# Graph network layer on one core: comparing dst rows group by group, and stores of the counts issued by ScalarE

## The reference

```
# layer 0: a message per edge, summed by dst
msg = relu(concat(x[dst], x[src], edge_attr, u) @ W1 + b1)
agg = segment_sum(msg, dst)
x   = layernorm(x + relu(concat(x, agg, u) @ W2 + b2))
# layers 1 and 2 (same edges)
h   = x @ W + b
agg = segment_sum(h[src] + edge_attr @ We + be, dst) + h
x'  = batchnorm(relu(agg) + bias)
# end
out = layernorm(x + layer 2 of layer 1 of x)
```

## Time and profile before

| | |
|---|---|
| median of 3 runs | 8024.89 us (8016.9 to 8026.22) |
| profiled execution, its own time | 8035.52 us |
| its span | 8033.7 us |
| mean granted TensorE clock | 0.78 |
| preparation, to the first sum of a tile | 0 to 266 us |
| tiles and counts | 266 to 4741 us |
| windows to nodes | 4741 to about 5390 us |
| layers 1 and 2 | about 5390 to 8034 us |

### The profile page before, as it was taken

How to read it: one execution, slowest core, us unless ns; L and a number is a source line. 1 busy time by engine, 2 the same in 40 slices (tenths; PEclk the granted TensorE clock), 3 DMA queues, 4 the chain that set the end, 5 groups by cost and what they waited for, 6 DMA issues and landing times.

```text
span 8033.7 us, 166672 instructions
## 1 busy us (share of the span) xinstructions
PE 6117.4 (76%) x60411; PEld 5242.1 (65%) x60411; DVE 4457.3 (55%) x5988; ACT 2089.5 (26%) x5280; POOL 3990.2 (50%) x3983
## 2 busy tenths in 40 slices
PE   3136777777777777777777747779999999999996
PEld 2025555555555555555555536679999999999996
DVE  2238888888888888888888838860011111001113
ACT  1014444444444444444444400000000000000001
POOL 3777777777777777777777754430011110001111
PEclk9996666666666666666666665569999999999998
DMA  5227777777777777777777764449999998999996
GB/s 117 54 61 223 246 240 243 250 242 251 247 242 244 249 249 246 247 246 242 248 252 244 248 175 149 151 170 382 380 363 382 382 382 345 378 361 382 382 384 247
DMA packets 973642, 2113.96 MB, mean 263 GB/s; under 512 B 668464, under 2 KB 758534, under 8 KB 859646
## 3 DMA queue, kind: packets, MB, share of 16 engines
q1 hardware_dynamic: 814200, 1844.92, 61.7%
q0 software_dynamic: 137664, 259.86, 13.6%
q10 hardware_dynamic: 21696, 8.08, 0.6%
HBM read 1457.70 MB, written 654.73 MB: 263 GB/s over the span
## 4 chain that ended last, share of the span: by engine, by line
PE 49%; DVE 19%; issue 12%; DMA 9%; POOL 8%; DVEq 1%; SPq 1%; ACT 1%; ACTq 0%; POOLq 0%
PE psum L947 25%; PE psum L836 10%; DVE edge_area L1322 9%; POOL arena L669 5%; PE psum L811 4%; PE psum L794 4%; DMA arena<-adj 4%; PE psum L795 2%; DVE arena L1313 2%; POOL arena L683 2%; DMA arena<-in_src_steps 1%; DVE edge_area L1327 1%; DMA arena<-b_tab,arena 1%; POOL arena L641 1%; DMA arena<-q_tab,m_window 1%
## 5 line engine op out<-in xcount | busy, mean ns | idle before, releaser
L669 POOL DMA_INDIRECT arena<-b_tab,arena x3125 | 3122.2, 999 | 952.2 <-issue 935.8
L1322 DVE TENSOR_TENSOR edge_area<-psum,arena 128x1024 bf16<-128x1024 f32 x2368 | 2484.6, 1090 | 622.1 <-PE psum L811 622.1
L1075 ACT CAST arena<-psum 128x392 bf16<-128x392 f32 x4736 | 1921.2, 505 | 2119.9 <-PE psum L811 2066.5
L947 PE MATMUL psum<-arena 128*128 128x192 bf16 x29008 | 2449.4, 246 | 29.0 <-DMA arena<-adj 20.7
L947 PEld LDWEIGHTS psum<-arena 128*128 128x128 bf16 x29008 | 2403.2, 98 | 38.3 <-issue 35.0
L811 PE MATMUL psum<-edge_area 64*128 64x98 bf16 x18944 | 1226.7, 241 | 464.9 <-ACT arena L1075 456.3
L794 PE MATMUL psum<-w_edge,arena 96*128 96x288 f32 x1250 | 677.3, 638 | 957.8 <-DVE arena L1313 957.8
L731 POOL DMA_INDIRECT arena<-a_carry,a_carried x196 | 185.0, 944 | 2404.3 <-DVE arena L1512 1374.5
L811 PEld LDWEIGHTS psum<-edge_area 64*128 64x128 bf16 x18944 | 782.6, 110 | 712.0 <-issue 684.7
L1478 DVE TENSOR_REDUCE arena<-psum 128x64 f32<-128x192 f32 x296 | 104.1, 352 | 1700.2 <-PE psum L947 1114.6
L794 PEld LDWEIGHTS psum<-w_edge,arena 96*128 96x128 f32 x1250 | 268.2, 267 | 1035.4 <-issue 1035.4
(11 more groups left out here) (248 smaller groups left out, 3263.7 us busy)
## 6 DMA issues: line engine op xcount, KB each, us to landing
arena<-adj SPq DMA_DIRECT2D x592, 1568.0 KB, 8.8
adj<-arena SPq DMA_DIRECT2D x296, 1568.0 KB
q_tab<-arena SPq DMA_DIRECT2D x312, 480.0 KB, 3.4
edge_area<-q_tab SPq DMA_DIRECT2D x117, 768.0 KB, 5.0
arena<-in_edge_t_steps SPq DMA_DIRECT2D x312, 192.0 KB
over_area<-q_tab SPq DMA_DIRECT2D x78, 768.0 KB
arena<-b_tab,arena POOLq DMA_INDIRECT x3125
over_area<-m_cont SPq DMA_DIRECT2D x196, 48.0 KB
```

Source lines behind the costliest of these rows:

```text
L669: nc.gpsimd.indirect_dma_start(rows[:, us, k, S - 1 - s, :], None, b_tab[:, :], bass.IndirectOffsetOnAxis(ap=index[:, us, 1 - k, s:s + 1], ...
L947: one = mm(psum[:, h, 0:3 * F], ring[:, r, n, :], xs[l][:, k, :], start=(k == 0 and not own), stop=(k == NB - 1))
L1075: copy(stage[:, h2, h, :, column:column + BATCH], psum[:, 2 + 2 * b + h, 0:BATCH * NB].rearrange("p (e n) -> p n e", n=NB)).then_inc(kept, 1)
L1322: one = V.tensor_tensor(to[:, d, :, :], over(lanes, [P, HOT, n], 1), over(code, [P, HOT, n], 2), ALU.is_equal)
```

## The change

Three things. DVE's preparation starts with the compares, unrolled, and puts the other parts behind single groups: the ends behind group 2, the masks behind 3 and 4, the flags behind 6, the products behind 7 and 8. PE makes the shift of the ends ahead of its own group 6 and turns the flags ahead of group 12, not behind all 14 groups. And the eight stores of counts in a cycle are issued by ACT, behind its copies of an odd step, not by SP; SP's loop loses them and one peeled cycle.

```diff
 # SP
-            def store_quarter(q, h, part): ... sp.wait_ge(kept, ...); sp.dma_start(adj..., stage...)
-            def store_quarters(c, uu, build_now, built_before): ...
             def tile_cycle(c):
 ...
                     over_unit(c, uu)
-                    store_quarters(c, uu, build_now, built_before)
-            tile_cycle(0, False, False)
-            tile_cycle(1, True, False)
-            with sp.Fori(2, BUILD + 1) as c:
-                tile_cycle(c, True, True)
+            tile_cycle(0)
+            with sp.Fori(1, BUILD + 1) as c:
+                tile_cycle(c)
 # PE
             for g in range(NG):
                 h = g % 2
+                if g == 6:
+                    shift_ends()     # waits for ends_known; 8 products, ends_ps_done
+                elif g == 12:
+                    turn_conts()     # waits for conts_known; 3 transposes, conts_turned
                 pe.wait_ge(xt_in[h], 16 * (g // 2 + 1))
 ...
-            pe.wait_ge(ends_known, 1)
-            ...                      # the same 8 products and 3 transposes
 # ACT
+            quarters_at = ((0, 1), (2,), (3,), ())
+            def store_quarter(q, h, part):
+                of, half = part // 2, slice(part % 2 * QH, (part % 2 + 1) * QH)
+                act.wait_ge(kept, q * (2 * PAIR_BATCHES) + 2 * PAIR_BATCHES)
+                act.dma_start(adj[of][some(q, 1), :, half.start * P:half.stop * P]...,
+                             stage[:, h, of, half, :]...).then_inc(adj_out[h], 16)
+            def store_quarters(c, uu, build_now, built_before):
+                if uu >= 4 and build_now:
+                    for part in quarters_at[uu - 4]:
+                        store_quarter(c * 2 - 2, 0, part)
+                if uu < 4 and built_before:
+                    for part in quarters_at[uu]:
+                        store_quarter(c * 2 - 3, 1, part)
             def keep_cycle(c, build_now=True, built_before=True):
                 for j in range(CYCLE):
                     if build_now:
                         keep_batches(c, j)
                     over_step(c, j)
+                    if j % 2:
+                        store_quarters(c, j // 2, build_now, built_before)
 # DVE
-            dve.wait_ge(dst_in, 64)
-            ...                      # ends, masks, dve.wait_ge(ends_ps_done, 1), flags, products
-            counted_loop(dve, count, 0, NG // 2, compare)
+            for g in range(NG):
+                compare(g)
+                if g == 2:
+                    ends_of_windows()          # waits for dst_in
+                elif g == 3:
+                    run_mask(m_mask, m_dst, m_ends, MOB, WM)
+                elif g == 4:
+                    run_mask(a_mask, a_dst, a_ends, AOB, WA)
+                elif g == 6:
+                    continuations()            # waits for ends_ps_done
+                elif g == 7:
+                    run_goes_on(m_mask, m_cond, MOB, WM)
+                elif g == 8:
+                    run_goes_on(a_mask, a_cond, AOB, WA)
```

More of the change, by code:

```diff
@@ L454, in _ @@
             sp.dma_start(a_cont[1:1 + AOB * P].rearrange("(b p) -> b p", p=P), cont_t[0:AOB, 2, :]).then_inc(conts_out, 16)
[L456 to L468, removed]
             q_windows = q_tab.rearrange("(w i) f -> w (i f)", i=WM)
             units_of = ((0, 1), (1, 2, 3), (3, 4), (4, 5, 6), (6, 7))
-            quarters_at = ((0, 1), (2,), (3,), ())
             def load_over(c, n):
@@ L522, in over_unit, with tile_cycle @@
                     load_cont(c, 3)
-            def tile_cycle(c, build_now, built_before):
+            def tile_cycle(c):
                 for uu in range(CU):
@@ L536, in tile_cycle @@
                     over_unit(c, uu)
-                    store_quarters(c, uu, build_now, built_before)
             sp.wait_ge(conts_out, 80)
-            tile_cycle(0, False, False)
-            tile_cycle(1, True, False)
-            with sp.Fori(2, BUILD + 1) as c:
-                tile_cycle(c, True, True)
-            tile_cycle(CYCLES - 1, False, True)
+            tile_cycle(0)
+            with sp.Fori(1, BUILD + 1) as c:
+                tile_cycle(c)
+            tile_cycle(CYCLES - 1)
             us = (UNITS - 1) % 4
@@ L758, in _, with shift_ends, turn_conts @@
             pe.wait_ge(globals_kept, 1)
+            def shift_ends():
+                pe.wait_ge(ends_known, 1)
+                for at, of, n in ((0, m_ends[:, 0, :], MOB), (MOB, m_ends[:, 1, :], MOB),
+                                  (2 * MOB, a_ends[:, 0, :], AOB), (2 * MOB + AOB, a_ends[:, 1, :], AOB)):
+                    mm(ends_ps[:, at:at + n], shift[:, :], of[:, 0:n], start=True, stop=False)
+                    one = mm(ends_ps[:, at:at + n], wrap[:, :], of[:, 1:n + 1], start=False, stop=True)
+                one.then_inc(ends_ps_done, 1)
+            def turn_conts():
+                pe.wait_ge(conts_known, 1)
+                nc.tensor.transpose(glob_ps[0:NB, 0:P], m_cont_p[:, 0:NB], ident[:, :])
+                nc.tensor.transpose(glob_ps[0:NB, P:2 * P], m_cont_p[:, NB:2 * NB], ident[:, :])
+                nc.tensor.transpose(glob_ps[0:AOB, 2 * P:3 * P], a_cont_p, ident[:, :]).then_inc(conts_turned, 1)
             for g in range(NG):
                 h = g % 2
+                if g == 6:
+                    shift_ends()
+                elif g == 12:
+                    turn_conts()
                 pe.wait_ge(xt_in[h], 16 * (g // 2 + 1))
@@ L1096, in over_step, with keep_cycle @@
                     over_keep(b + (j - 10) // 3)
-            def keep_cycle(c, build_now=True):
+            quarters_at = ((0, 1), (2,), (3,), ())
+            def store_quarter(q, h, part):
+                of, half = part // 2, slice(part % 2 * QH, (part % 2 + 1) * QH)
+                act.wait_ge(kept, q * (2 * PAIR_BATCHES) + 2 * PAIR_BATCHES)
+                act.dma_start(adj[of][some(q, 1), :, half.start * P:half.stop * P].rearrange("k p n -> (k p) n"),
+                             stage[:, h, of, half, :].rearrange("p n c -> p (n c)")).then_inc(adj_out[h], 16)
+            def store_quarters(c, uu, build_now, built_before):
[5 more added lines that the diff above has]
+                        store_quarter(c * 2 - 3, 1, part)
+            def keep_cycle(c, build_now=True, built_before=True):
                 for j in range(CYCLE):
@@ L1102, in keep_cycle @@
                     over_step(c, j)
+                    if j % 2:
+                        store_quarters(c, j // 2, build_now, built_before)
             act.wait_ge(codes_kept, AP_ // 2)
             act.wait_ge(codes_turned, AP_ // 2)
-            keep_cycle(0, False)
-            keep_cycle(1)
+            keep_cycle(0, False, False)
+            keep_cycle(1, True, False)
             with act.Fori(2, BUILD + 1) as c:
@@ L1262, in _, with ends_of_windows @@
-            counted_loop(dve, count, 0, NG // 2, compare)
+            def ends_of_windows():
+                dve.wait_ge(dst_in, 64)
+                for of, ends, n in ((m_dst, m_ends, MOB), (a_dst, a_ends, AOB)):
+                    note(V.tensor_copy(ends[:, 0, 0:n], of[:, :, 0]))
+                    note(V.tensor_copy(ends[:, 1, 0:n], of[:, :, of.shape[2] - 1]))
+                count.wait()
+                V.tensor_scalar(m_target[:, :], m_ends[:, 1, 0:MOB], 0.0, None, ALU.max).then_inc(ends_known, 1)
@@ new lines, in run_mask, with continuations @@
+            def run_mask(mask, of, ends, n, w):
+                note(V.tensor_tensor(mask[:, 0:n, :], of, over(ends[:, 1, 0:n], [P, n, w], 2), ALU.is_equal))
+            def continuations():
+                dve.wait_ge(ends_ps_done, 1)
+                note(V.tensor_tensor(m_cond, ends_ps[:, 0:MOB], m_ends[:, 1, 0:MOB], ALU.is_equal))
+                note(V.tensor_tensor(m_cont_p, ends_ps[:, MOB:2 * MOB], m_ends[:, 1, 0:MOB], ALU.is_equal))
+                note(V.tensor_tensor(a_cond, ends_ps[:, 2 * MOB:2 * MOB + AOB], a_ends[:, 1, 0:AOB], ALU.is_equal))
+                V.tensor_tensor(a_cont_p, ends_ps[:, 2 * MOB + AOB:2 * (MOB + AOB)], a_ends[:, 1, 0:AOB], ALU.is_equal)\
+                    .then_inc(conts_known, 1)
@@ new lines, in run_goes_on, with compare @@
+            def run_goes_on(mask, cond, n, w):
+                count.wait()
+                note(V.tensor_tensor(mask[:, 0:n, :], mask[:, 0:n, :], over(cond, [P, n, w], 2), ALU.mult))
+            def compare(g):
+                h = g % 2
+                wait(dve, rows_compared, g)
+                dve.wait_ge(tile_rows_in[h], (g // 2 + 1) * (16 * GB))
+                link(V.tensor_tensor(is_less, tile_rows[:, h, :, :],
+                                     over(node[:, g * GB:(g + 1) * GB], [P, GB, P], 2), ALU.is_lt))
+                V.tensor_reduce(t[5][:, g * GB:(g + 1) * GB], is_less, AX.X, ALU.add).then_inc(rows_compared, 1)
```

## The result

The changed kernel takes 8075.99 us (median of 4 runs, 8072.17 to 8080.99) against 8025.56 us (8016.9 to 8028.64, 4 runs): a ratio of 1.0065, its 95% interval 1.0048 to 1.0082. It is slower by 50 us where 64 us less had been forecast, and far outside the range of 7940 to 7995.

What follows compares the result with a forecast made beforehand. POOL's list of gathers was taken to pace the first 4740 us, its 78 us hole paid in full. Compares first gained 64 us, stores on ACT 0: 8024.9 - 64 = 7961 us, range 7940 to 7995.

Steps and rivals of the forecast that it cites:

- Part 1: Preparation, compares first: POOL's gap before group 2 closes and source gathers start at 168.4 us, 64.0 us earlier.
- 105.0 us from group 1 to the source gathers: Preparation: 84 unhindered gathers at 1.25 us each, following group 1, so source gathers could start at 154.0 us.
- the holds: Preparation: DVE's four long operations now run beside POOL's gathers and hold them up, 8.2 to 13.2 us, taken as 12.4.
- the two more microseconds: Preparation: DVE's compares hold up POOL's gathers, bounds 0 to 17.5 us, taken as 2.
- Group 0 was in time: Preparation: group 0's rows might land as late as 54.28 us, costing POOL 7.5 us; taken as 0.
- 8.8 us for the compares: Preparation: by the skill page's contention rule every compare could hold a gather, 8.8 us, a gain of 57, not 64.
- Part 2: Count stage: ACT issues the stores in place of SP; bounds -17 to +136 us, taken as 0.
- The landings: Count stage: with stores in their own queue gathers land later; DVE would wait 4.1 us more, once, giving 7965.
- the queues served in turns: DMA engines take turns between busy queue rows; a third would give gathers every third turn in place of every second.
- POOL as the pace: First 4740 us: POOL gathers without a pause and sets the pace, so a hole in its list is paid in full.
- Rival 1: Count stage: ACT's store issues delay its copies, then PE and DVE; full price 136 us, 8097 us; chance 0.05.
- The signs that I named for part 2 going wrong: Count stage: ACT's idle after steps 5 and 11 near 0, DVE's idle before line 1322 longer, POOL waiting for sums or indices.

Runs made afterwards that it cites:

- earlier: Changed kernel, stores still on ACT, but each half's last quarter issued behind steps 3 and 11 instead of 5 and 13; 7955.17 us, ratio 0.9913 to the kernel before.
- stores_only: Kernel before with only the stores moved to ACT (SP and ACT as changed, PE and DVE as before); 8134.25 us, ratio 1.0136.
- half1_earlier: Changed kernel with only the second half's last quarter store moved from behind step 5 to behind step 3; 7968.17 us, ratio 0.9936 to the kernel before.
- sp_ahead: Kernel before with the new preparation, stores on SP, the second half's last quarter directly ahead of the window's load; 8075.57 us, ratio 1.0065.

## Why the prediction was wrong

**Part 1, right in each of its terms.** The 105.0 us from group 1 to the source gathers, the holds and the two more microseconds gave 168.4; measured 168.15. The four long operations held 2.96 + 3.27 + 3.21 + 3.27 = 12.7 us (the rows of 72.72 to 125.67 less 0.94 each); I took 12.4. Group 0 was in time: its compare started at 44.10, ahead of the 54.28 of the bound. For the compares I took 2 us: POOL started 0.24 us earlier than before (31.15 against 31.39), 154.0 - 0.24 + 12.7 = 166.5, and 1.7 us remain to 168.15. The page "GPSIMD Engine Reference" of the Trainium skill, section "8. Key points", says that POOL's SBUF interfaces contend with DVE's instructions of two SBUF inputs; the prediction made 8.8 us for the compares of it. The trace bears it out for all four long operations, and for the compares in small part (the 1.7 us).

**Part 2, the step that failed.** I wrote of SP's eight issues that in "a cycle from SP, whose DMAs nobody in the loop waits for" they go at gain 0, and set the whole part to 0 "since every idle stretch there is longer than its issues". The second half is true as far as it goes: ACT's idle is as long as it was, and `earlier` shows the issues to be free. The first is wrong: DVE's operation on a window needs SP's load of it, and saw no wait only because the load had landed by then; that POOL hardly waits for indices says nothing of DVE. And the step priced the instruction and not the transfer. A store of 1568 KB takes the DMA engines for microseconds (93% of them in the 3.3 us shown above), and what mattered is who comes behind it. On SP the store stood behind the load of the window by the order of the code (`store_quarters` is the last line of the unit), and on ACT, which waits for nothing there, it comes ahead of it. I had listed the queues and counted the issues, and had not laid ACT's time after step 5 beside SP's load in the timeline. The idle stretch of ACT that ends at 2056.43 is in the earlier trace rows and was used as room for a store; the load at 2055.54 falls into that same stretch, and DVE's operation at 2061.32 needs it. The issue did not even go into that stretch: in after it stands ahead of it, among step 5's copies. The term was 0; it measured 111 us in the profiled execution and 109.3 in `stores_only`: 3.41 in the steady cycle, of which 2.42 are step 7's longer time and 0.99 stand in other steps. Over all 37 cycles it is 3.0 on average, since some early cycles of before were longer than 109.23 too.

**The landings.** I weighed gathers landing later (4.1 us once, 7965). DVE's waits for rows did rise, with the stores on ACT in good places, to 25.9 us in 3000 in `earlier`, and the kernel still is the fastest. I had the queues served in turns; in the 3.3 us shown above ACT's store got 93% of the engines, POOL's gathers 5% and SP's queue nothing, though the trace does not show when SP's load had packets ready. And I looked at gathers alone; the transfer whose slack ran out was the load of a window, one of the five in a cycle.

**POOL as the pace.** "POOL's list of gathers paces the first 4740 us" is half of it. The prediction also said that the ring of DVE, PE and ACT runs at nearly the same pace and that the stage could not "stay the same if that ring becomes slower", and this is what happened. POOL in after waits once a cycle up to 3.9 us:

```profile
POOL arena L652 <- issue: 1033.5, 3080, 3.9
```

It now runs ahead of the ring until something on its side holds it, perhaps indices that SP loads or sums that SP stores (not tested). I take it for a consequence: DVE has no wait for gathered rows there, and in `half1_earlier` nothing of POOL was changed, and its longest wait goes back to 0.3 us.

**The rivals.** Rival 1 had the sign, the part and, by luck, about the size (136 us against 109), and the wrong mechanism: its price was ACT's time, and that is covered. It got 0.05. The signs that I named for part 2 going wrong were ACT's idle near 0, DVE's idle ahead of the one-hot rows, and POOL waiting. The first did not come. DVE's idle grew by about 1 us a cycle and POOL waits, but the loss begins at neither; the sign that decides, DVE waiting for a window, was on no list.

## What to carry to other kernels

When a DMA issue moves to another engine, its own instruction is the small part: write down what stood ahead of it and behind it in the old queue, at what time the new engine will reach it, and which transfer with a waiting reader then comes behind it. A large store that nobody waits for belongs behind the load that somebody waits for, or far enough ahead of it, in whichever queue. A freer engine issues earlier, and earlier can be worse: here the store cost nothing one unit earlier or 3 us behind the load, and 3.4 us in each cycle at 2 us ahead of it.

## What the runs showed of the hardware

- The order of two transfers counts across queues: DVE started 7.9 us after the load's issue with the store 2.1 us ahead of it in another queue, and 8.45 us after it with the store 0.5 us ahead in the same queue. A separate queue gave the load no protection: with 1.00 MB of the store under way in ACT's queue, SP's queue started no packet in the 3.3 us behind the load's issue.
- An issue by SP took longer behind the large store: `arena<-in_src_steps` took 0.40 us at 2056.09 before, ahead of the store, and 3.06 at 2060.14, behind it; after, behind the store, 1.16 at 2020.23 and 2.06 at 2024.81. What that costs was not tested.
- A gather that POOL starts under one of DVE's long operations ended 0.81 to 0.82 us after that operation, four times of four (76.62 against 75.80 us for the first), and took 3.90 to 4.21 us and not 0.94.
- One wait of 2.4 us in each cycle of a ring of DVE, PE and ACT cost 3.4 us: by the starts of DVE's sums (medians of 24 cycles) the step with the wait is 2.4 us longer and three later ones 0.44, 0.24 and 0.18. With the wait at 3.2 us, in `sp_ahead`, the cycle lost the same 3.4, and without it all came back.
